# Four linears whose first pieces are split a stage earlier, and a routing that ranks whole rows of gates

## The reference, cut to what matters

```
edge_index = jnp.stack([src, dst])
xn = _layernorm(x, axis=-1)
x = x + _L0_gnn_ref(xn, ...) + _L0_mix_ref(xn[None], ...)[0]        # mix ends in: out @ Wo + bo
x = x + _L0_ffn_ref(_layernorm(x, axis=-1)[None], ...)[0]
xn = _layernorm(x, axis=-1)
x = x + _L1_gnn_ref(xn, src, dst, ...) + _L1_mix_ref(xn[None], ...)[0]   # mix ends in: attn @ Wo.T + bo
x = x + _L1_ffn_ref(_layernorm(x, axis=-1)[None], ...)[0]

def _L0_ffn_ref(...):                              # the first routing: each expert takes its best 391 nodes
    topw, topi = jax.lax.top_k(probs, K)           # K = 2 of 8 experts
    gates = jnp.zeros((T, E), x.dtype).at[jnp.arange(T)[:, None], topi].set(topw)
    top_g, tok_idx = jax.lax.top_k(gates.T, cap)

def _sage_layer(...):                              # twice in the second layer
    agg = jax.ops.segment_sum(msg, edge_dst, num_segments=h.shape[0])
    mean = agg * deg_inv[:, None]                  # deg_inv = 1.0 / jnp.maximum(deg, 1.0)
    return h @ W_self + mean @ W_neigh + b
```

## Time and profile before

| | us |
|---|---|
| median of three runs | 3314.9 |
| the runs | 3305.74 to 3317.59 |
| the profiled execution's own time | 3312.88 |
| span of that execution | 3311.2 |
| mean granted share of TensorE's clock | 0.954 |
| TensorE / VectorE / ScalarE / GpSimd busy | 3055.6 / 2038.9 / 1264.8 / 457.8 |

### The profile page before, as it was taken

How to read it: one execution, slowest core, us unless ns; L and a number is a source line. 1 busy time by engine, 2 the same in 40 slices (tenths; PEclk the granted TensorE clock), 3 DMA queues, 4 the chain that set the end, 5 groups by cost and what they waited for, 6 DMA issues and landing times.

```text
span 3311.2 us, 53342 instructions
## 1 busy us (share of the span) xinstructions
PE 3055.6 (92%) x22308; PEld 2807.6 (85%) x22308; DVE 2038.9 (62%) x3622; ACT 1264.8 (38%) x2163; POOL 457.8 (14%) x328
## 2 busy tenths in 40 slices
PE   6999999989998799999599999989998999979998
PEld 6998897389977498988599997989998999978887
DVE  6986477977876645544556564776355643645665
ACT  4453055444421134433254343444134421424554
POOL 1033444444000111201000000000000000002222
PEclk9999999999998799999799999999999999968999
DMA  8322122132052256746611011353321333147997
GB/s 254 114 57 42 1 30 42 1 78 55 6 144 97 59 154 178 194 130 163 164 61 39 27 37 32 116 148 80 79 79 63 96 87 95 54 138 227 264 264 213
DMA packets 261921, 344.44 MB, mean 104 GB/s; under 512 B 40706, under 2 KB 223016, under 8 KB 259988
## 3 DMA queue, kind: packets, MB, share of 16 engines
q1 hardware_dynamic: 163351, 191.08, 19.4%
q0 software_dynamic: 43312, 77.14, 11.9%
q10 hardware_dynamic: 54989, 72.35, 7.3%
HBM read 264.10 MB, written 76.40 MB: 103 GB/s over the span
## 4 chain that ended last, share of the span: by engine, by line
PE 58%; DVE 4%; ACT 1%; DMA 1%; ACTq 1%; issue 1%; POOL 0%; DVEq 0%; POOLq 0%
PE PV L461 13%; PE PV L463 12%; PE PV L462 12%; PE PV L565 5%; PE PS L461 3%; PE PS L462 3%; PE PS L463 3%; PE PA L602 1%; PE PA L489 1%; DVE b_split L1747 1%; ACT b L1287 1%; PE PA L897 1%; PE PV L888 1%; PE PV L909 1%; PE PS L915 1%
## 5 line engine op out<-in xcount | busy, mean ns | idle before, releaser
L461 PE MATMUL PV<-WH,b_split 128*125 128x256 f32 (+2 forms) x3708 | 1088.1, 293 | 118.9 <-DVE b_split L1653 101.9
L462 PE MATMUL PV<-WH,b_split 128*125 128x256 f32 (+2 forms) x3708 | 1074.9, 290 | 0.0
L463 PE MATMUL PV<-WH,b_split 128*125 128x256 f32 (+2 forms) x3708 | 1074.2, 290 | 0.0
L1653 DVE TENSOR_TENSOR b_split<-b,b_split 128x500 fp32r<-128x500 f32 x1040 | 689.9, 680 | 431.0 <-ACT b_split L1276 417.3
L1276 ACT CAST b_split<-b 128x500 fp32r<-128x500 f32 x1040 | 627.2, 613 | 807.1 <-PE PV L463 731.2
L461 PEld LDWEIGHTS PV<-WH,b_split 128*125 128x125 f32 (+2 forms) x3708 | 701.1, 189 | 143.4 <-issue 100.7
L462 PEld LDWEIGHTS PV<-WH,b_split 128*125 128x125 f32 (+2 forms) x3708 | 703.5, 190 | 9.9
L463 PEld LDWEIGHTS PV<-WH,b_split 128*125 128x125 f32 (+2 forms) x3708 | 700.5, 189 | 11.3
L1636 DVE TENSOR_TENSOR WH<-WS,WH 128x1024 fp32r<-128x1024 f32 x292 | 344.6, 1222 | 128.1 <-ACT WH L1261 126.8
L1261 ACT CAST WH<-WS 128x1024 fp32r<-128x1024 f32 x292 | 291.9, 1051 | 162.0 <-PE PV L565 141.1
L461 PE MATMUL PV<-b_split,WH 128*128 128x250 f32 (+3 forms) x1136 | 335.9, 296 | 7.5 <-DVE b_split L1653 6.4
(11 more groups left out here) (275 smaller groups left out, 3598.6 us busy)
## 6 DMA issues: line engine op xcount, KB each, us to landing
WS<-in_L_ffn_w SPq DMA_DIRECT2D x46, 1024.0 KB
WH<-at_d SPq DMA_DIRECT2D x15, 1093.8 KB
WS<-in_L_ffn_gate_w SPq DMA_DIRECT2D x16, 1024.0 KB
WS<-in_L_ffn_up_w SPq DMA_DIRECT2D x16, 1024.0 KB
WS<-in_L_ffn_down_w SPq DMA_DIRECT2D x16, 1024.0 KB
b<-key_d POOLq DMA_DIRECT2D x4, 2560.0 KB, 9.2
WS<-in_L_mix_Wv SPq DMA_DIRECT2D x8, 1024.0 KB
WS<-in_L_mix_Wk SPq DMA_DIRECT2D x8, 1024.0 KB
```

The source lines that it names most:

```text
L461: pe.matmul(o, a[0], b[0], start=start, stop=False, **kw)
L462: pe.matmul(o, a[0], b[1], start=False, stop=False, **kw)
L463: return pe.matmul(o, a[1], b[0], start=False, stop=stop, **kw)
L1653: ve.tensor_tensor(lo, src, hi.bitcast(F32), ALU.subtract).then_inc(xl_done, 1)
```

## The change

Four parts. (1) Before wo0 three, before wo1, wn0 and wn1 four pieces are split ahead of the stage's end: hi_piece and lo_piece are called where the columns they read are done, and the linear starts with `first=`. For wo0 they stand on VectorE between the 23rd and the 24th attention step; for wo1 on ScalarE ahead of its last two copies; for wn0 and wn1 on VectorE ahead of the fifth chunk's weight quarter. TensorE no longer waits for the 24th step. (2) The reciprocal of the degrees is made on 125 by 10 values in the graph convolution's linear (`dmean`), and stored in place of the degrees. (3) In the first routing the gates are split into a high and a low fp32r part, and a row group is 1250 columns in three neighbouring banks, PV for even and PS for odd ones, each bank from two fp32r products with 8 rows. VectorE reads the columns ahead of the own group and those from it on in one instruction each. (4) GpSimd's zeroing of gT is gone.

```diff
@@ first pieces @@
-            pe.wait_ge(acc_free, KD * 3)
             linear_rows("wo0")
...
+            act.wait_ge(acc_free, KD * 3 - 2)
+            act.wait_ge(qp_used, 4 * (KD - 2) * 3)
+            for src in row_pieces(B1)[0:EARLY - 1]:
+                hi_piece(src)
             act.wait_ge(acc_free, KD * 3)
-            linear_residual(B1, A["x"])
+            linear_residual(B1, A["x"], first=EARLY - 1)
...
                 act.copy(cols(B1)[:, pr, c0:c0 + cn], s.read(act)[:, 0:cn]).then_inc(s_free, 1)
+                if m == 3 * KD - 3:
+                    act.wait_ge(s_free, s.n)
+                    for src in row_pieces(B1)[0:EARLY]:
+                        hi_piece(src)
...
-            linear_residual(B1, x2_d, store=(xm_d, xm_stored))
+            linear_residual(B1, x2_d, store=(xm_d, xm_stored), first=EARLY)
...
+            act.wait_ge(v_free, mark["agg1"] - 4 * KD)
+            for src in row_pieces(B3)[0:EARLY]:
+                hi_piece(src)
             act.wait_ge(v_free, mark["agg1"])
...
-            linear_residual(B3, hs_d)
+            linear_residual(B3, hs_d, first=EARLY)
...
-            for step in range(KD * 3):
+            for step in range(KD * 3 - 1):
                 attend(step)
+            ve.wait_ge(acc_free, KD * 3 - 1)
+            for src in row_pieces(B1)[0:EARLY - 1]:
+                lo_piece(src)
+            attend(KD * 3 - 1)
             ve.wait_ge(acc_free, KD * 3)
-            lo_pieces(row_pieces(B1), add_residual(B3, True))
+            lo_pieces(row_pieces(B1), add_residual(B3, True), first=EARLY - 1)
...
                         emptied(ve.tensor_tensor(cols(B3)[:, f, c * AC:(c + 1) * AC], v.read(ve)[:, 0:AC],
                                                  degs[:, c * AC:(c + 1) * AC], ALU.mult))
+                    if c == T // AC - 2:
+                        for src in row_pieces(B3)[0:EARLY]:
+                            lo_piece(src)
@@ degrees @@
+                    d(ve.tensor_scalar(dmean[0:R, :], dcol[0:R, :], 1.0, None, ALU.max))
+                    d.sync()
+                    ve.reciprocal(dmean[0:R, :], dmean[0:R, :]).then_inc(dg_in, 1)
...
-            ve.wait_ge(dinv_in, 16)
-            d(ve.tensor_scalar(degs, degs, 1.0, None, ALU.max))
-            d.sync()
-            d(ve.reciprocal(degs, degs))
@@ routing @@
             for n in range(2 * NT):
                 k, i = divmod(n, NT)
+                if n >= 2:
+                    pe.wait_ge(rank_used, rank_ops[n - 2])
                 for c0 in range(0, T, HALF):
                     cn = min(HALF, T - c0)
-                    pe.matmul(v.take(pe)[0:R, 0:cn], gT[:, 1 + k, i * R:(i + 1) * R], gT[:, 0, c0:c0 + cn],
-                              start=True, stop=True).then_inc(v_full, 1)
+                    for part in range(2):
+                        mm = pe.matmul(choice_gates(n)[0:R, c0:c0 + cn], gatesT[:, 2 + k, i * R:(i + 1) * R],
+                                       gatesT[:, part, c0:c0 + cn], start=(part == 0), stop=(part == 1))
+                mm.then_inc(rank_full, 1)
+            pe.wait_ge(rank_used, rank_ops[2 * NT - 1])
...
+                    d(ve.tensor_copy(gatesT[:, 0, at], bank))
+                    d.sync()
+                    emptied(ve.tensor_tensor(gatesT[:, 1, at], bank, gatesT[:, 0, at].bitcast(F32), ALU.subtract))
...
+                gates, own, g = choice_gates(n)[0:R, :], i * R, wk[0:R, k, i:i + 1]
+                seen, seen_own = rank_scratch(n)
+                ve.wait_ge(rank_full, n + 1)
+                if n >= 2:
+                    ve.wait_ge(rank_used, rank_ops[n - 2])
+                if i:
+                    ve.tensor_scalar(seen[:, 0:own], gates[:, 0:own], g, None, ALU.is_ge, ALU.add,
+                                     accum_out=rk[:, 0, k, i:i + 1]).then_inc(rank_used, 1)
+                ve.scalar_tensor_tensor(out=seen_own, in0=gates[:, own:own + R], scalar=g, in1=low[0:R, 0:R],
+                                        op0=ALU.is_equal, op1=ALU.mult,
+                                        accum_out=rk[:, 2, k, i:i + 1]).then_inc(rank_used, 1)
+                ve.tensor_scalar(seen[:, own:T], gates[:, own:T], g, None, ALU.is_gt, ALU.add,
+                                 accum_out=rk[:, 1, k, i:i + 1]).then_inc(rank_used, 1)
```

More of the change, by code:

```diff
@@ L305, in edge_batches, with choice_gates, rank_scratch @@
             return max(0, j - NPIECE) * (GROUPS // 4) // ((NQ - 1) * NPIECE)
+        gatesT = FR[0:E, B2:B2 + 4 * T].rearrange("p (a t) -> p a t", t=T)
+        rank_ops = [3 * (n + 1) - (n // NT + 1) for n in range(2 * NT)]
+        def choice_gates(n):
+            return (PV, PS)[n % 2].rearrange("p a b -> p (a b)")[:, 0:T]
+        def rank_scratch(n):
+            at = B2 + 8400 + T // 2 * (n % 2)
+            own = B2 + 8400 + T + P * (n % 2)
+            return F[0:R, at:at + T // 2].bitcast(BF16), F[0:R, own:own + R]
         def ffn_shape(layer):
@@ L1263, in next_unit, with hi_piece, hi_pieces @@
                 n_unit[0] += 1
-            def hi_pieces(views, lead=None, extra=None):
-                for j, src in enumerate(views):
+            def hi_piece(src):
+                g = n_piece[0]
+                n_piece[0] += 1
+                if g >= 4:
+                    act.wait_ge(*xs_end[g - 4])
+                hi = split_ring(g)[0].rearrange("p (k t) -> p k t", k=src.shape[1])
+                act.copy(hi, src).then_inc(xh_done, 1)
+            def hi_pieces(views, lead=None, extra=None, first=0):
+                for j, src in list(enumerate(views))[first:]:
                     if lead and j < NPIECE and j % 4 == 0:
@@ L1604, in norm_1 @@
                     ln_sqrt(b)
-            linear_residual(B3, xs_d, also=norm_1)
+            linear_residual(B3, xs_d, also=norm_1, first=EARLY)
             for j in (NQ * NPIECE, NQ * NPIECE + 4):
@@ L1640, in next_unit, with lo_piece, lo_pieces @@
                 n_unit[0] += 1
-            def lo_pieces(views, evac, lead=None, after=None):
-                for j, src in enumerate(views):
+            def lo_piece(src):
+                g = n_piece[0]
+                n_piece[0] += 1
+                hi, lo = (h.rearrange("p (k t) -> p k t", k=src.shape[1]) for h in split_ring(g))
+                ve.wait_ge(xh_done, g + 1)
+                ve.tensor_tensor(lo, src, hi.bitcast(F32), ALU.subtract).then_inc(xl_done, 1)
+            def lo_pieces(views, evac, lead=None, after=None, first=0):
+                for j, src in list(enumerate(views))[first:]:
                     if lead and j < NPIECE and j % 4 == 0:
@@ L2157, in _ @@
                     w = min(4, NT - 4 * g) * R
-                    emptied(ve.tensor_copy(gT[:, a, 4 * g * R:4 * g * R + w], v.read(ve)[0:E, 0:w]))
+                    at, bank = slice(4 * g * R, 4 * g * R + w), v.read(ve)[0:E, 0:w]
+                    if a:
+                        emptied(ve.tensor_copy(gatesT[:, 1 + a, at], bank))
+                        continue
+                    d(ve.tensor_copy(gatesT[:, 0, at], bank))
+                    d.sync()
+                    emptied(ve.tensor_tensor(gatesT[:, 1, at], bank, gatesT[:, 0, at].bitcast(F32), ALU.subtract))
             nself = sm("nself", E, 160)
@@ L2171, in _ @@
                 k, i = divmod(n, NT)
-                for c0 in range(0, T, HALF):
-                    cn = min(HALF, T - c0)
-                    ve.wait_ge(v_free, v.n)
-                    d.sync()
[L2176 to L2194, removed]
@@ L2201, in _ @@
             d(ve.tensor_tensor(rank, rk[:, 0, :, :], rk[:, 1, :, :], ALU.add))
-            for a in range(2, 7):
-                d.sync()
-                d(ve.tensor_tensor(rank, rank, rk[:, a, :, :], ALU.add))
+            d.sync()
+            d(ve.tensor_tensor(rank, rank, rk[:, 2, :, :], ALU.add))
             d.sync()
@@ L2265, in _ @@
                 emptied(ve.tensor_scalar(RB[:, n % 4, 0:cn], v.read(ve)[:, 0:cn], 0.0, 0.125, ALU.max, ALU.mult))
-            lo_pieces(row_pieces(B1), add_residual(B3, True))
+            for src in row_pieces(B1)[0:EARLY]:
+                lo_piece(src)
+            lo_pieces(row_pieces(B1), add_residual(B3, True), first=EARLY)
             residual_done()
-            ve.wait_ge(dinv_in, 16)
-            d(ve.tensor_scalar(degs, degs, 1.0, None, ALU.max))
-            d.sync()
-            d(ve.reciprocal(degs, degs))
             def evac_own(m):
@@ L2288, in means @@
                                                  degs[:, c * AC:(c + 1) * AC], ALU.mult))
+                    if c == T // AC - 2:
+                        for src in row_pieces(B3)[0:EARLY]:
+                            lo_piece(src)
             d.sync()
             split_rows()
+            ve.wait_ge(dinv_in, 16)
             ve.wait_ge(xm_stored, BOTH * NQ * NB)
             means()
-            lo_pieces(row_pieces(B3), add_residual(B1, False, relu=True))
+            lo_pieces(row_pieces(B3), add_residual(B1, False, relu=True), first=EARLY)
```

(2 more changed lines are left out.)

42 lines of the change are left out of this document (16 added, 26 removed).

## The result

| | before | after |
|---|---|---|
| median of the runs, us (6 each, one chip) | 3314.4 | 3287.0 |
| the runs | 3302.8 to 3327.6 | 3277.8 to 3294.4 |
| the profiled execution's own time | 3312.9 | 3287.0 |
| its span, and TensorE's mean granted clock | 3311.2, 0.954 | 3285.1, 0.949 |

The ratio is 0.9926, 95% interval 0.9907 to 0.9945: faster by 0.7%, 27 us where I had forecast 40. The kernels further on were each timed beside new runs of the kernel before (medians 3309.5 to 3313.5); each ratio is to those, so that ratios compare them better than medians. I compared the two traces where TensorE ends one stage and begins the next. The stretches that answer to the earlier trace rows: us, busy time of PE, PEld, DVE, ACT, POOL (x count), PEclk, DMA.

The account below looks back on a forecast made before the run. TensorE (58% of the span) was taken to bound, losing time in stops and at half clock. Savings of 12.6 + 1.8 + 5.5 + 6.6 + 7.2 + 6.7 = 40.4 us took 3314.9 to 3274; 8-in-10 range 3262 to 3291.

Parts of the forecast that it names:

- the likeliest case: The forecast itself for the whole kernel: median 3274 us, 65% chance, own range 3264 to 3284.
- Routing, -12.6: First routing's counts: twenty row groups of 1.85 us, 36.7 in place of 50.2, less added gate copies; net -12.6 us.
- if TensorE keeps up: Routing: condition that TensorE makes a group's 2 x 1250 fp32r columns in 1.17 us, under VectorE's 1.85.
- The rival of the falling clock: Routing: short TensorE stops of 0.7 us each group halve its clock, 2.33 us a group, 3284 us; 15%.
- wn0 and wn1, -7.2 and -6.7: Neighbours' sums and their linears: early-split pieces let the fifth piece be reached 7.2 and 6.7 us sooner.
- it goes from the chunk straight into four pieces: Before wn0: TensorE runs from the fifth chunk into four early pieces, 5.7 us, while ScalarE issues residual loads.
- The added wait in the fifth chunk: Before wn0: VectorE's four low parts delay emptying the fifth chunk's first bank, so TensorE waits 1.1 us.
- wo0, -1.8: Before wo0: stops of 2.0 and 6.3 us; gain 3.9 less about 2.1 for half clock behind the second.
- wo1 and ws0, -5.5 and -6.6: wo1: early pieces, stops 0.7 and 1.6 us, no half clock; ws0: low part 7.2 earlier, stop 3.8, half clock remains.
- no stop over 1 us between the sum and the linear: Sign expected in the profile after, before wn0 and wn1, beside one stop of 1.1 us in the fifth chunk.
- The slow fp32r products (3333): Rival, routing: fp32r products run at the plain float32 rate, 4.8 us a group, 59 us more, 3333 us; 3%.
- the empty early pieces (3295.7): Rival: early pieces before the four linears give nothing; only routing and ws0 remain, 19.2 us, 3295.7; 13%.

## Why the prediction was partly wrong

- The time, 3287.0, lies in the range (3262 to 3291) and on the side that had 93%, but 13 us above the forecast and outside the likeliest case's own 3264 to 3284. Three terms of the sum fell short by 16 us; the others gave back 2. That the range held it is partly luck: one of the two mechanisms behind the shortfall stood among the rivals, with another reason, and the other nowhere.
- **Routing, -12.6, got -5.0.** VectorE's side was right: 1.51 us for a count of 1250 columns (forecast 1.52), 1.84 a group once TensorE keeps up. The step that failed is "if TensorE keeps up": I took 0.467 ns a column from products of 128 rows for products of 8, having written that no row has one, and kept the clock at 1.00. The rival of the falling clock had the effect (2.33 us a group, it is 2.24 to 2.34) and nearly the time, 3284. Its reason was wrong: TensorE was to fall by standing still 0.7 of 1.85 us. The rule of the Trainium skill that I cited with it ("TensorE: Matmul & The Clock Gate", section "A second HAM failure mode: psum-queue depth-cycling"), by which such short stops can swing the clock, is not borne out here: with 128 rows the stops at each change of banks are there, 0.44 us every 1.84, and PEclk is 1.00.
- **wn0 and wn1, -7.2 and -6.7, got -1.3 and -4.0.** The step that failed is "it goes from the chunk straight into four pieces": TensorE stopped for 1.51 and 2.50 us before wn0 and 1.78 before wn1. No semaphore held it there, and the stops go when nothing is left to jump over. That the same delay was hidden before by the stop of 6.2 us is my inference. The jump could be read off the program: it stood exactly where I took a stop away. With the branches exchanged the terms come out at -7.0 and -8.3. The added wait in the fifth chunk was 0.69 us (forecast 1.1). The sum itself became 2.1 and 2.2 us longer: 0.69 is that wait, and the half clock at its start covers 9.1 us of its products where it covered 6.8, some 1.1; I had no term for this.
- **wo0, -1.8, got -3.0.** Both stops came, the first as forecast (2.12 for 2.0). The clock fell behind it too, which I had not taken: the three pieces took 6.01 us for 4.3, and that shortened the second stop to 4.28 from 6.3, for the fourth piece came within 0.3 us of the time given, counted from the attention's last product. The half clock behind the second stop, 3.4 us of it (some 1.6 lost), is what I had at 2.1.
- **wo1 and ws0, -5.5 and -6.6, got -5.9 and -6.0**, with the stops as described. For ws0 the phase at half clock behind the stop lasted 5.45 us, some 25 products, where before it was 14: 1.0 us dearer. I had named that 1 us and taken only 0.6 of it off.
- Of the signs that were to prove the forecast wrong, a row group of over 2.1 us came true (2.24 to 2.34), and the second stop before wn0 stood at its mark of 2.5 us. The sign "no stop over 1 us between the sum and the linear" failed at both.
- The slow fp32r products (3333) and the empty early pieces (3295.7) did not happen.

## What to carry to other kernels

A product with few rows may halve TensorE's clock however busy it is; before a contraction is cut from 128 rows to the ones that hold data, compare the time at half clock with the other engine's, and fill up with zeros if TensorE would become the bound. When a stop is taken away, ask what else it hid: a jump over code (with it, as I read it, the fetch of instructions) is named by no semaphore, and only shows once nothing else is late. In this kernel the branch that is taken stood better last where work follows at once, and first where a big load was under way at its start; the second rests on one place. Then look at stages that the edit did not touch, since stops came and went there too.

## What the runs showed of the hardware that I had not expected

- PEclk 0.50 to 0.51 (1.2 GHz) with 8, 32 and 64 rows at 96 to 100% busy, and 1.00 (2.4 GHz) with 128 rows, of which 120 are zero, at 74% busy (27.89 of 37.80 us).
- With 8 rows the clock fell from 1.00 3.7 us into the stretch, in which TensorE had not stopped (3.67 us busy).
- With a jump over the float32 branch in front of work that is ready, TensorE stood 1.5 and 2.5 us before wn0 and 1.8 before wn1, and 7.4 us at one place beside a load of 1.1 MB. Without the jump these stops are gone.
- Leaving out code elsewhere brought three stops of 2.1 to 2.9 us into a stage that the edit did not touch. A fourth there, of 2.5 to 3.1 us, came and went with six other edits. No semaphore ends them.
